# Attention with 16 heads of 64: scores of two heads in 64-row tiles, read straight from the projections

## What is computed

```python
xn = layer_norm(x, g1, b1)                 # the context, n = 375 rows
ln_lat = layer_norm(latents, g2, b2)       # l = 112 rows
q = ln_lat @ Wq                            # 256 -> 16 heads x 64
kv = jnp.concatenate([xn, ln_lat], axis=1) @ Wkv     # 487 rows
k, v = jnp.split(kv, 2, axis=-1)
weight = jnp.einsum('bhld,bhnd->bhln', q * scale, k * scale)   # 112 x 487 per head
weight = softmax(where(full_mask, weight, neg))
out = jnp.einsum('bhln,bhnd->bhld', weight, v)
return out @ Wout
```

## Time and profile before

| | |
|---|---|
| median of 3 runs | 1531.09 us (1529.65 to 1533.0) |
| the profiled execution | 1528.29 us, its span 1526.3 us |
| granted clock over the span, mean | 0.953 |
| PE busy | 1357.1 us (89%) |
| DVE busy | 1177.2 us (77%) |
| ACT busy | 954.2 us (63%) |
| POOL busy | 654.9 us (43%) |
| middle stage, first scores to last | 525.0 to 1285.7 us |

### The profile page before, as it was taken

One profiled execution on the slowest core, in us unless ns is written; L12 is line 12 of the kernel. 1 busy time (PEld: TensorE's weight loads), 2 busy tenths in 40 slices (PEclk: granted clock), 3 DMA queues, 4 the chain that ended last, 5 costly groups with the idle time before them and its releaser, 6 DMA issues. The chain is left out here.

```text
span 1526.3 us, 45153 instructions
## 1 busy us (share of the span) xinstructions
PE 1357.1 (89%) x14276; PEld 1053.6 (69%) x14276; DVE 1177.2 (77%) x3350; ACT 954.2 (63%) x2456; POOL 654.9 (43%) x1044
## 2 busy tenths in 40 slices
PE   5999999999974799999999999999999997279995
PEld 3788888888751367776776677767766776278994
DVE  4899999999863388887887877878878787267772
ACT  4887888888951366665666665656656666045663
POOL 3544444444543234342543344334534424235654
PEclk8999999999976899999999999999999999589998
DMA  5333333333201666346653565447634671473323
GB/s 163 100 117 115 115 101 115 115 111 97 72 8 34 130 135 127 88 90 129 144 110 69 120 144 108 91 94 145 125 80 96 130 160 48 136 287 55 61 40 73
DMA packets 167807, 163.36 MB, mean 107 GB/s; under 512 B 81274, under 2 KB 155394, under 8 KB 164528
## 3 DMA queue, kind: packets, MB, share of 16 engines
q1 hardware_dynamic: 151440, 118.80, 34.2%
q0 software_dynamic: 13168, 35.80, 9.3%
q10 hardware_dynamic: 3024, 6.47, 1.5%
HBM read 64.48 MB, written 41.96 MB: 70 GB/s over the span
## 5 line engine op out<-in xcount | busy, mean ns | idle before, releaser
L1414 PE MATMUL b_ps_p<-b_tok_s,w_s 128*128 128x112 f16 (+1 forms) x1536 | 223.3, 300 | 11.3 <-DVE b_k_s L1698 6.6
L1709 DVE CUSTOM_DVE_ANT_0 b_prob<-b_ps_s,b_keep 112x487 f32<-112x487 f32 x256 | 167.9, 656 | 27.4 <-PE b_ps_s L1493 26.3
L1414 PE MATMUL b_ps_p<-w_s,b_tok_s 128*122 128x512 f16 x768 | 186.9, 379 | 0.0
L1605 ACT ACTIVATE b_prob<-b_prob,b_top 112x487 f32<-112x487 f32 x256 | 177.6, 694 | 10.5 <-DVE b_top L1709 10.3
L1414 PEld LDWEIGHTS b_ps_p<-b_tok_s,w_s 128*128 128x128 f16 x1536 | 117.5, 100 | 95.9 <-issue 17.9
L1611 ACT ACTIVATE b_pT<-b_ps_t 122x448 f16<-122x448 f32 x256 | 137.7, 538 | 72.1 <-PE b_ps_t L1501 69.6
L1493 PE MATMUL b_ps_s<-b_k_stack,b_q_dup 128*112 128x487 f16 x512 | 153.4, 382 | 25.6 <-issue 15.9
L1714 DVE TENSOR_TENSOR b_pT<-b_ps_t,b_pT 122x448 f16<-122x448 f32 x256 | 158.6, 619 | 6.9 <-ACT b_pT L1611 5.5
L701 ACT ACTIVATE a_prob<-a_prob,a_top 112x375 f32<-112x375 f32 x256 | 156.4, 611 | 4.4 <-DVE a_top L837 3.4
L837 DVE CUSTOM_DVE_ANT_0 a_prob<-a_ps_s,a_keep 112x375 f32<-112x375 f32 x256 | 138.2, 540 | 24.4 <-PE a_ps_s L593 21.8
L1521 PEld LDWEIGHTS b_ps_o<-b_v_s,b_pT 122*128 122x128 f16 x3072 | 122.5, 98 | 44.3 <-issue 6.6
(11 more groups left out here) (259 smaller groups left out, 3062.1 us busy)
## 6 DMA issues: line engine op xcount, KB each, us to landing
b_k_stack<-b_k_s SPq DMA_DIRECT2D x64, 487.0 KB, 11.0
xs<-a_blank SPq DMA_DIRECT2D x14, 1032.0 KB, 4.0
b_q_dup<-b_q_s SPq DMA_DIRECT2D x128, 112.0 KB, 5.2
c_w_pool<-w_split SPq DMA_DIRECT2D x8, 1600.0 KB, 10.5
b_wch_f<-in_w_experts POOLq DMA_DIRECT2D x32, 384.0 KB, 11.8
w_split<-b_wch_s POOLq DMA_DIRECT2D x32, 384.0 KB, 7.2
a_ctx_f<-in_ctxT SPq DMA_DIRECT2D x16, 375.0 KB, 3.7
a_k_stack<-a_k_s SPq DMA_DIRECT2D x64, 93.8 KB, 2.8
```

The costliest lines, as they stand in the source:

```text
L1414: last = pe.matmul(out, sta(a, k), mov(m, k), start=(k == 0 and n == 0), stop=(k == tiles - 1 and n == 2))
L1605: act.activation(prob[:, h % RING, 0:NK], prob[:, h % RING, 0:NK], ACT.Exp, bias=top[:, h % RING:h % RING + 1], scale=-1.0, accum_out=sums ...
L1709: dve.tensor_tensor_reduce(prob[:, h % RING, 0:NK], ps_s[h % 2][0:T, 0:NK], keep[par][:, :], -SCALE1, 3e38, ALU.add, ALU.min, top[:, h % R ...
```

## The change

Scores are no longer made from stacked copies. `k_stack`, `q_dup`, their DMAs and their two semaphores go; `k_s` and `q_s` get two buffers and are read directly. Heads 2p and 2p+1 lie in the lower and upper 64 partitions of the same tile of `k_s` and `q_s`, so one call of `scores` now does both: three passes, and in each a matmul on rows 0 to 63 for the even head into `ps_s[0]` and one on rows 64 to 127 for the odd head into `ps_s[1]`. The product LO·LO is no longer made. It is called in even slots alone, behind `transposes` instead of ahead of them, and needs the maxima of both heads of the pair before. `s_score` counts pairs.

```diff
-        q_s = sb("q_s", [128, 2, IT, T], F16)
-        q_dup = [sb(f"q_dup{i}", [128, 2, H, T], F16) for i in range(2)]
-        k_s = sb("k_s", [128, 2, IT, NK], F16)
-        k_stack = [sb(f"k_stack{i}", [128, H, NK], F16) for i in range(2)]
+        q_s = [sb(f"q_s{i}", [128, 2, IT, T], F16) for i in range(2)]
+        k_s = [sb(f"k_s{i}", [128, 2, IT, NK], F16) for i in range(2)]
...
-            def stack(c, par):
-                need_all(sp, settled, (s_ihi, PI, c, P_Q), (s_ifree, PI, c, P_Q), (s_score, H, c - 1, 1))
-                for a in range(2):
-                    for part in (HI, LO):
-                        src = k_s[64 * a:64 * a + 64, part, :, :]
-                        rows = part if a == 0 else 1 - part
-                        sp.dma_start(k_stack[par][64 * rows:64 * rows + 64, a::2, :], src).then_inc(s_kstack, 16)
-                need_all(sp, settled, (s_ihi, PI, c, P_V), (s_ifree, PI, c, P_V))
-                for a in range(2):
-                    for rows in range(2):
-                        for part in (HI, LO):
-                            sp.dma_start(q_dup[par][64 * rows:64 * rows + 64, part, a::2, :],
-                                         q_s[64 * a:64 * a + 64, part, :, :]).then_inc(s_qdup, 16)
...
-            def scores(b, par, h):
-                if h == 0:
-                    need(pe, s_qdup, 128, b, 128)
-                    need(pe, s_kstack, 64, b, 64)
-                need(pe, s_max, H, b, h - 1)
-                for part in (HI, LO):
-                    last = pe.matmul(ps_s[h % 2][0:T, 0:NK], q_dup[par][:, part, h, :], k_stack[par][:, h, :],
-                                     start=(part == HI), stop=(part == LO))
+            def scores(b, par, pair):
+                if pair == 0:
+                    need(pe, s_ihi, PI, b, P_V)
+                    need(pe, s_ifree, PI, b, P_V)
+                need(pe, s_max, H, b, 2 * pair)
+                for n, (a, m) in enumerate(PASSES):
+                    for half in range(2):
+                        rows = slice(64 * half, 64 * half + 64)
+                        last = pe.matmul(ps_s[half][0:T, 0:NK], q_s[par][rows, a, pair, :], k_s[par][rows, m, pair, :],
+                                         start=(n == 0), stop=(n == 2))
                 last.then_inc(s_score, 1)
...
                 for s in range(H):
-                    scores(b, par, s)
                     if not (first(b) and s < 2):
                         c, _, h = behind(s, 2, b, par)
                         transposes(c, h)
+                    if s % 2 == 0:
+                        scores(b, par, s // 2)
...
             def maxima(b, par, h):
-                need_all(dve, settled, (s_score, H, b, h + 1), (s_tr, H, b, h - RING + 1), *([(s_keep, 1, b, 1)] if h == 0 else []))
+                need_all(dve, settled, (s_score, H // 2, b, h // 2 + 1), (s_tr, H, b, h - RING + 1), *([(s_keep, 1, b, 1)] if h == 0 else []))
```

More of the change, by code:

```diff
@@ L1106, in phase_attention_large_heads @@
         s_ifree = sem("ifree")
-        s_kstack = sem("kstack")
-        s_qdup = sem("qdup")
         s_score = sem("score")
@@ L1213, in body @@
                     load(b + 2)
-                if ahead(b, 1):
-                    stack(b + 1, 1 - par)
                 if not first(b):
@@ L1220, in _ @@
             load(1)
-            stack(0, 0)
             run_batches(sp, body)
@@ L1581, in item @@
                 if k < P_Q:
-                    if k == 0:
-                        need(act, s_kstack, 64, c, 0)
-                    act.activation(k_s[:, HI, k, :], ps[:, 0:NK], ACT.Copy).then_inc(s_ihi, 1)
+                    act.activation(k_s[par][:, HI, k, :], ps[:, 0:NK], ACT.Copy).then_inc(s_ihi, 1)
                 elif k < P_V:
                     j = 4 * (k - P_Q)
-                    if j == 0:
-                        need(act, s_qdup, 128, c, 0)
-                    act.activation(q_s[:, HI, j:j + 4, :], ps[:, 0:4 * T].rearrange("p (j n) -> p j n", j=4), ACT.Copy).then_inc(s_ihi, 1)
+                    act.activation(q_s[par][:, HI, j:j + 4, :], ps[:, 0:4 * T].rearrange("p (j n) -> p j n", j=4), ACT.Copy).then_inc(s_ihi, 1)
                 else:
@@ L1697, in item @@
                 if k < P_Q:
-                    dve.tensor_tensor(k_s[:, LO, k, :], ps[:, 0:NK], k_s[:, HI, k, :], ALU.subtract).then_inc(s_ifree, 1)
+                    dve.tensor_tensor(k_s[par][:, LO, k, :], ps[:, 0:NK], k_s[par][:, HI, k, :], ALU.subtract).then_inc(s_ifree, 1)
                 elif k < P_V:
                     j = 4 * (k - P_Q)
-                    dve.tensor_tensor(q_s[:, LO, j:j + 4, :], ps[:, 0:4 * T].rearrange("p (j n) -> p j n", j=4), q_s[:, HI, j:j + 4, :], ALU.subtract).then_inc(s_ifree, 1)
+                    dve.tensor_tensor(q_s[par][:, LO, j:j + 4, :], ps[:, 0:4 * T].rearrange("p (j n) -> p j n", j=4), q_s[par][:, HI, j:j + 4, :], ALU.subtract).then_inc(s_ifree, 1)
                 else:
```

## The result

The changed kernel takes **1536.5 us** (median of 7 runs, 1532.99 to 1541.75), the one before 1529.94 (7 runs, 1528.93 to 1533.0): ratio 1.004, 95% interval 1.0023 to 1.0056. It is slower by 0.4%. The forecast was 1519, faster; the range of 1501 to 1548 holds the time, on the side of the third rival. The profiled execution took 1532.99 us, its span 1531.4; it is the fastest of the seven.

The account below looks back on a forecast made before the run. PE was taken to bound the middle stage, a plain slot being the sum of what it issues. Start +10.3, shorter slots +3.0, last batch -1.5 gave 11.8 us off 1531.1: 1519 us, range 1501 to 1548.

Parts of the forecast that it names:

- the third rival: Even slots, batches 0 to 14: PE runs empty at every change of tile shape, 1539 to 1567 us; chance 0.25.
- Part 2: Score matmuls: a pair's six run side by side, 0.61 us plus D, against 0.87 before.
- D: What a pair's six score matmuls cost beyond 0.61 us: 0.15 taken, bounds 0 to 0.60.
- the fourth rival: Score matmuls: the array halves do not run side by side, 1.22 us a pair, about 1565 us; chance 0.08.
- 1.25: Gain in us per batch from shorter slots, five pairs at 0.23 plus 0.1, before D is charged in seven pairs.
- Parts 3 and 4: Shorter slots gain 3.0 us over fifteen batches; transposes first costs 0 there and 1.5 us in batch 15.
- hidden, 0: Transposes first, batches with projections: DVE has the odd head's maximum before PE asks, so 0 us lost.
- In slots 6 to 14 PE has no waits: Slots 6 to 14: PE does not wait and DVE is far from full, so five pairs pay in full, 0.23 us each.
- Part 1: Copies removed: 10.3 us gained at the start, slot 1 at 519.2 instead of 529.57; nothing in later batches.
- nothing queued behind the copies gates PE: SP's queue: SP's loads run two batches ahead, so removing the copies gives no further gain or loss there.
- Part 4: Batch 15, without projections to cover: every second maximum waits for scores, 1.5 us lost, within 0 to 3.4.
- the free tiles: Score matmuls in row tiles: D is 0.03 or less, 25 to 28 us gained, about 1504 us; chance 0.22.

Follow-up runs that it names:

- the probe: Kernel before, plus one unread 8-column matmul on rows 0 to 63 behind each head's two score matmuls: 1594.9 us (same on all 128 rows: 1544.57).
- the start-alone kernel: Kernel before, but batch 0 alone reads its scores in 64-row tiles without copies, later batches using stacks as before: 1517.8 us, ratio 0.9935.
- the kernel with unread copies: Changed kernel with all twelve copies a batch still issued on SP's queue into one stack that nobody reads: 1546.42 us.

## Why the prediction was wrong

**The sum per batch, step by step.** Each line is one kernel's inner batch against another's:

| step | kernels | us a batch |
|---|---|---|
| transposes ahead of scores | 47.66 to 47.73 | +0.07 |
| heads in pairs | 47.73 to 48.54 | +0.81 |
| three full-row matmuls instead of four | 48.54 to 46.63 | -1.91 |
| 64-row tiles instead of full rows | 46.63 to 48.41 | +1.78 |
| together | 47.66 to 48.41 | +0.75 |

The prediction had -0.20 in the place of +0.75. The saving that the change is built on is there: in the even slots that are free of waits (4, 8, 10 and 14) three matmuls in place of four give 0.21 to 0.23 a pair, where 0.87 - 0.61 = 0.26 was counted. Two costs ate it.

The steps are not independent. Slot 9's wait for `xn` is there with stacked pairs (2.76 us), gone with three full-row matmuls (2.26) and back with the tiles (2.66), so 0.5 of the 1.91 and 0.4 of the 1.78 are this one wait; another 0.35 of the 1.91 is slot 2 (4.66 to 4.31).

**Part 2, D: the step that failed first.** The split of D was a load's stagger of 0.05 and 0.05 for each way in and out. Both pieces were wrong. The stagger is nothing: PE in two narrow windows around 554.5 and 555.3 us of the changed kernel reads

```profile
554.34 0.26 PE L1481 MATMUL b_ps_t<-b_const,b_prob 112*122 112x112 f32 x1
554.53 0.41 PE L1473 MATMUL b_ps_s<-b_k_s,b_q_s 64*112 64x487 f16 x2
```

```profile
554.99 0.37 PE L1473 MATMUL b_ps_s<-b_k_s,b_q_s 64*112 64x487 f16 x2
555.28 0.64 PE L1391 MATMUL b_ps_p<-w_s,b_tok_s 128*122 128x512 f16 x2
```

Two matmuls of a pass stand in one line with one start; in the trace they start 3 to 4 ns apart, and the next pass 0.21 to 0.25 later. So the halves do run side by side, as forecast, and the fourth rival is dead. The Trainium skill (TensorE: Matmul & The Clock Gate, section on packing small matmuls) has 4 ns there; this trace agrees. The seams are what costs, about 0.14 each where 0.05 was taken: from the last transpose to the first scores 0.19 us where a plain hand-over before took 0.10, and from the last pass to the projection 0.29 where it took 0.20. With 0.05 behind each seam for a weight load that is no longer hidden that is 0.28, as between the two kernels above; the probe has 0.23 for a change there and back. The Trainium skill (TensorEngine Tiling (Array Packing), key properties) says that a change of mode drains the engine; that each change costs agrees with it, but the matmul behind a seam starts 0.07 us before the modelled end of the one ahead of it (554.34 + 0.26 against 554.53), so these traces do not show a full drain. I gave this rival 0.25 because no row of before showed a seam. The absence of one in the earlier trace rows said nothing, since every matmul there has more than 64 rows. The remaining 0.08 of D is no seam: four transposes directly behind the values take 0.41 to 0.43 (e.g. 557.39 - 556.98), behind scores 0.39, in both slots, and in slots 12 and 14 three full-row matmuls took 0.66, not 0.61.

The forecast for the third rival at D = 0.34 was 1539, and 1536.5 was measured. The agreement is better than its reasoning. I had built 0.34 of two pipeline tails of 0.17; the seams are shorter than that, and exposed loads and transposes fill the rest. And its sum, 7 x 0.34 - 1.25 = 1.13 a batch, charged D in seven pairs, of which three (slots 0, 6 and 12) have waits that take up part of it, and the pairing at nothing; the two errors partly cancel to 0.75.

**Parts 3 and 4, "hidden, 0": the step that failed second.** The order was priced by one question, whether the maxima are ready when PE asks. They nearly are: PE waits for `b_top` in one plain slot, 12, of every second batch, 0.2 us. But a slot that loses its scores is 0.4 shorter, and the work of the other engines that was hidden under it is not. The slots, by the runs (us, before then after):

| slots | before | after | | why |
|---|---|---|---|---|
| 15, 0 | 5.32 | 5.39 | +0.07 | exponentials of head 14; forecast 0 |
| 1 to 4 | 14.67 | 14.67 | 0 | DVE sets it, as forecast |
| 5, 6 | 4.60 | 4.30 | -0.30 | a wait of 0.3 for `ctx_n` in slot 6 fills up |
| 7, 8 | 7.76 | 7.83 | +0.07 | D |
| 9, 10 | 5.44 | 5.92 | +0.48 | 0.4 wait for `xn` |
| 11, 12 | 4.93 | 5.28 | +0.35 | 0.24 more in slot 12, the maximum |
| 13, 14 | 4.94 | 5.02 | +0.08 | D |

"In slots 6 to 14 PE has no waits" was wrong both before (slot 6: 0.3 us between the values, which take 0.35, and the transposes of `ctx_n`) and after (9 and 12). The wait in slot 9 can be followed on DVE in the changed kernel:

```profile
894.24 0.69 DVE L1682 TENSOR_TENSOR b_v_s<-b_ps_p,b_v_s 122x512 f16<-122x512 f32 x1 [0.70 <-ACT b_v_s L1570]
894.85 0.69 DVE L1668 TENSOR_SCALAR b_tok_f<-b_ps_o,b_affine 128x112 f32<-128x112 f32 x2
895.45 0.82 DVE L1736 TENSOR_SCALAR b_xn<-b_x,b_mv,b_rstd 112x256 f32<-112x256 f32 x1
```

and on PE:

```profile
896.42 0.38 PE L1441 MATMUL b_ps_o<-b_const,b_xn 112*128 112x112 f32 x2 [0.24 <-DVE b_xn L1736]
```

Slot 8's projection ends later in its slot, behind six score matmuls; DVE stands 0.70 us for its v item, although it has time to spare on average, then `xn` comes at the queue's end. My bound, 3.9 of 4.9 us of DVE work in two slots, was a share over the pair; the deadline lay inside the short one.

The order alone does not make the wait. `xn` lasts 0.82 us here, and 0.41 in the kernel before:

```profile
949.69 0.41 DVE L1759 TENSOR_SCALAR b_xn<-b_x,b_mv,b_rstd 112x256 f32<-112x256 f32 x1
```

Beside it GpSimd splits the tokens, in the changed kernel and in the one before:

```profile
895.27 0.85 POOL L1247 TENSOR_TENSOR b_tok_s<-b_tok_f,b_tok_s 128x375 f16<-128x375 f32 x1
949.98 0.85 POOL L1270 TENSOR_TENSOR b_tok_s<-b_tok_f,b_tok_s 128x375 f16<-128x375 f32 x1
```

Before, the split begins 0.29 us behind `xn`; now it begins 0.18 ahead of it, and `xn` ends 0.15 behind the split. The 13 profiles have 208 of these normalisations. 91 of them last longer than 0.42 us, up to 1.01, and every one of the 91 ends 0.13 to 0.16 us behind the end of a GpSimd instruction that ran as it began, or began within 0.04 us of it. With 0.41 us `xn` would have ended at 895.86, and PE, which starts 0.15 behind it, would have had it at 896.01, when the issue of the values ends (895.66 + 0.35): by this estimate from the rows, no wait. So the later order used up the slack, and the 0.4 is DVE's instruction held while GpSimd's ran. The run with three full-row matmuls a pair agrees: `xn` lasts 0.41 in its inner batches and slot 9 has no wait. But no run changes this alone: moving the normalisation up took 0.43 a batch off, and there `xn` also lasts 0.46 only.

**Part 1, the start: right, with one reason missing.** Slot 1 starts 10.3 us sooner, as computed: in the start-alone kernel item 0 begins at 515.71 and lasts 2.47, so slot 1 begins 15.6 us behind the v items, before 25.95. The clock stayed at its upper level (1.00 from 515 to 528 us). The start alone gives 11.6 us between medians (1529.4 in its comparison), of which 9.9 is seen by the end of batch 1. What failed is the sentence that nothing queued behind the copies gates PE. It holds in the inner batches; at the start the load of batch 2 would have taken the wait's place, as the kernel with unread copies shows. The 10.3 needed both, the wait gone and the queue free.

**Part 4, the last batch: right in kind.** -1.5 taken, -2.1 measured, within the 0 to 3.4 given. It is not the tiles: with three full-row matmuls a pair it was 32.26, of which 1.1 is the clock (slot 4 takes 3.10 us against 2.04, at a mean granted clock of 0.56 from 1241.6 to 1244.8), so about the same without it. The pairing alone, with stacks, gave 29.92; what makes up the rest was not tried.

**Sum, with measured terms:** 10.3 gained at the start, of which the rest of batches 0 and 1 give 1.7 back (0.4 of it already in the start-alone kernel), 10.2 lost in batches 2 to 14 and 2.1 in the last: 10.3 - 1.7 - 10.2 - 2.1 = -3.7 in the stage. The signs of the start, the last batch, slots 15 to 4 and the side-by-side passes were right. The forecast of the whole failed on D and on the free order: the tiles cost 1.78 a batch where 7 x 0.15 = 1.05 was taken, the pairing 0.81 where 0 was. Two slips in the working change nothing in it: by its own sums the free tiles end at 1503, not 1501, and the fourth rival at 1567, not 1565.

## What to carry to other kernels

A row tile saves columns and pays at each change of tile shape: count the changes there and back, 0.22 to 0.29 us here, against the columns saved in between (here 0.21 to 0.23 us a pair), and take it only where a run of matmuls in one shape is long enough, or where it removes a wait, as in batch 0 here. When work is gathered from every slot into every second one, look at the slots that get shorter: for each engine, what must be ready inside the short slot, not its share over both, and which instructions of DVE and GpSimd now meet. And before taking away the wait that ended last, look for what stood in the same queue behind it; here it would have held PE almost as long.

## What the runs showed of the hardware that was not expected

- A change between 128-row and 64-row tiles costs about 0.1 us, in either direction, even for a matmul of 8 columns (0.23 there and back in a plain slot); two such changes cost 0.22 to 0.29 us between long matmuls.
- A DVE normalisation (112x256, float32) of 0.40 us that begins while a GpSimd instruction runs can be held until 0.15 us behind its end: 0.82 us in the changed kernel, up to 1.01 with the 64-row probe.
- Matmuls in the two 64-row halves start 3 to 4 ns apart though each has its own weights, and a pass of two takes 0.21 to 0.25 us, about what one of 487 columns takes.
- Four float32 transposes directly behind values (64-column matmuls) last 0.02 to 0.04 us longer than behind scores. What causes it was not tried.
- DMA copies that move 45 MB in the stage cost PE nothing in mid-stage (48.39 against 48.41 an inner batch), and 10 us once, where a load stood behind them.
- PE stands 2.8 to 4.7 us at each end of a loop body in the 13 profiles, and in most cases the clock is at its lower level for some us behind it; the batches with such an end took 51.0 to 54.5 us in the changed kernel, the others 48.4 to 48.6.
